# Layer 2's dot features: halves made in node order and turned by one transposing transfer

## The reference, cut to what matters

```python
def _gat_layer(h, mask, b):
    scores = jnp.einsum('...nd,...md->...nm', h, h)
    scores = jnp.where(mask, scores, NEG)
    attn = jax.nn.softmax(scores, axis=-1)
    return jnp.einsum('...nm,...md->...nd', attn, h) + b
h = jnp.einsum('bnc,hdc->bhnd', x, Wh)
out_h = _gat_layer(h, mask[None, None], bh[None, :, None, :])
cat = jnp.transpose(out_h, (0, 2, 1, 3)).reshape(B, N, H * D)
z = jax.nn.leaky_relu(cat, negative_slope=0.2)
h2 = jnp.einsum('bnk,dk->bnd', z, Wo)
out2 = _gat_layer(h2, mask[None], bo)
```

## Time and profile before

| | us |
|---|---|
| median of three runs | 2002.39 (1998.01 to 2004.02) |
| profiled execution | 2003.45 |
| its span in the profile | 2001.6 |
| outside the span | 1.85 |
| mean granted TensorE clock | 0.991 |

### The profile page before, as it was taken

One profiled execution on the slowest core, in us unless ns is written; L12 is line 12 of the kernel. 1 busy time (PEld: TensorE's weight loads), 2 busy tenths in 40 slices (PEclk: granted clock), 3 DMA queues, 4 the chain that ended last, 5 costly groups with the idle time before them and its releaser, 6 DMA issues.

```text
span 2001.6 us, 95064 instructions
## 1 busy us (share of the span) xinstructions
PE 1906.4 (95%) x43624; PEld 1566.2 (78%) x43624; DVE 1681.5 (84%) x1991; ACT 1242.2 (62%) x1886; POOL 1008.6 (50%) x726
## 2 busy tenths in 40 slices
PE   7998898989999999999999999999999999989998
PEld 6787798977777777777777777777777777767887
DVE  6999988767788888888888888888888888867998
ACT  5887655436666666666666666666666666654342
POOL 6676866412354455445454454455435455354653
PEclk8999999999999999999999999999999999999999
DMA  7000000011111111111111111111111111101111
GB/s 182 4 4 4 2 2 2 2 25 33 34 34 35 34 35 34 35 34 31 36 29 32 35 34 35 34 35 34 35 32 29 36 31 34 35 13 25 25 25 35
DMA packets 88255, 61.24 MB, mean 31 GB/s; under 512 B 45616, under 2 KB 86832, under 8 KB 87856
## 3 DMA queue, kind: packets, MB, share of 16 engines
q1 hardware_dynamic: 85632, 54.57, 11.2%
q10 hardware_dynamic: 2224, 0.59, 0.1%
HBM read 8.98 MB, written 4.19 MB: 7 GB/s over the span
## 4 chain that ended last, share of the span: by engine, by line
PE 70%; DVE 14%; ACT 6%; POOL 5%; issue 2%; DMA 1%; SPq 1%; ACTq 0%; POOLq 0%; DVEq 0%
PE ACC L1632 30%; PE S L1813 23%; PE S L1792 6%; DVE ring L1406 5%; PE AX L1856 3%; DVE ring L1259 2%; PE AX L1865 2%; PE AX L1833 2%; POOL sp_log L782 1%; POOL ln_sq L785 1%; ACT ring L1059 1%; DMA FA<-lo 1%; PE AX L1612 1%; DVE ch_rden L1391 1%; ACT st_x L898 1%
## 5 line engine op out<-in xcount | busy, mean ns | idle before, releaser
L1632 PEld LDWEIGHTS ACC<-V,ring 128*64 128x64 f32 x28672 | 955.4, 138 | 179.6 <-DVE ring L1259 34.6
L1406 DVE TENSOR_TENSOR ring<-ring,mask_self_t 128x1024 f32<-128x1024 f32 x640 | 896.0, 1410 | 193.2 <-ACT ring L1059 188.8
L1632 PE MATMUL ACC<-V,ring 128*64 128x65 f32 x28672 | 974.0, 223 | 29.1 <-ACT accs L870 11.9
L1059 ACT ACTIVATE ring<-S,dot_bias 128x1024 f32<-128x1024 f32 x640 | 713.7, 1116 | 414.1 <-PE S L1813 376.0
L1813 PE MATMUL S<-FA 128*64 128x512 f16 x5120 | 666.0, 382 | 4.7 <-DMA FA<-lo 4.6
L1813 PEld LDWEIGHTS S<-FA 128*64 128x64 f16 x5120 | 253.7, 110 | 164.7 <-ACT ring L1059 16.0
L1259 DVE SCALAR_TENSOR_TENSOR ring<-S,pair_q,mask_t 128x1024 f32<-128x1024 f32 x256 | 315.2, 1273 | 15.4 <-DVE f_max L1271 4.6
L798 POOL TENSOR_TENSOR EV_both<-score,recip 128x512 f32<-128x512 f32 x64 | 124.3, 1942 | 323.2 <-DVE score L1415 323.1
L1792 PE MATMUL S<-parts,mask_t 128*128 128x128 bf16 x3072 | 176.1, 221 | 10.8 <-DVE X L1395 10.6
L1792 PEld LDWEIGHTS S<-parts,mask_t 128*128 128x128 bf16 x3072 | 175.0, 99 | 11.8 <-issue 11.8
L791 POOL TENSOR_TENSOR V<-v_pairs,bh_bc 128x512 f32<-128x512 f32 x64 | 95.5, 1493 | 120.8 <-ACT v_pairs L1079 120.8
(11 more groups left out here) (134 smaller groups left out, 2044.2 us busy)
## 6 DMA issues: line engine op xcount, KB each, us to landing
FA<-hi SPq DMA_DIRECT2D x320, 64.0 KB, 2.0
FA<-lo SPq DMA_DIRECT2D x320, 64.0 KB, 2.0
X<-in_x SPq DMA_DIRECT2D x16, 256.0 KB, 5.0
ring<-in_adj SPq DMA_DIRECT2D x8, 512.0 KB, 8.1
out_x<-X SPq DMA_DIRECT2D x16, 256.0 KB, 2.6
wh<-in_wh_t ACTq DMA_DIRECT2D x2, 64.0 KB, 6.5
bh_bc<-in_bh ACTq DMA_DIRECT2D x1, 128.0 KB, 9.4
w_gat<-in_w_gat ACTq DMA_DIRECT2D x4, 16.0 KB, 3.8
```

Source lines behind the costliest of these rows:

```text
L1059: act.activation(ring[:, jt, :], S[jt % 2][:, :], ACT.Exp, bias=dot_bias[:, n % 2:n % 2 + 1])\
L1406: dve.tensor_tensor(ring[:, jt, :], ring[:, jt, :], mask_self_t[:, jt, :], ALU.mult)\
L1632: last = pe.matmul(acc_of(t)[rows, :], ring[:, jt, t * P + c * CUT:t * P + (c + 1) * CUT], values, start=(jt == 0 and t % 4 == 0), stop=(j ...
```

## The change

Both halves are made in node order, with nodes on the partitions, in one array `HL` of 128 x 8 tiles x (64 `hi` + 64 `lo`). ACT makes `hi` in step 0, straight from `AX`, ahead of the copy to `v_pairs`. DVE makes `lo` in step 1, from `v_pairs` and `hi`, ahead of the norms. SP issues one transposing transfer of 256 KB that writes plane 0 of `FA`, waits for it, and copies its two partition halves crosswise to plane 1, 128 KB each. The four turns on PE, ACT's step-2 copy, DVE's step-3 subtraction and the bank job `F` are gone.

```diff
-        hi = sb("hi", [P, 2, HALF], F16)
-        lo = sb("lo", [P, 2, HALF], F16)
+        HL = sb("HL", [P, 2, T, 2 * D], F16)
...
-            return 16 * 8 * (u["n"] // 2 + 1)
+            return 16 * 2 * (u["n"] // 2 + 1)
...
             for u in UNITS:
                 par = buf_of(u)
-                moved = features_in[par]
-                sp.wait_ge(hi_made, u["n"] + 1)
-                for half in range(2):
-                    cols_of = slice(half * HALF, (half + 1) * HALF)
-                    own = slice(half * D, (half + 1) * D)
-                    sp.dma_start(FA[0:D, par, 0, cols_of], hi[own, par, :]).then_inc(moved, 16)
-                    sp.dma_start(FA[D:P, par, 1, cols_of], hi[own, par, :]).then_inc(moved, 16)
                 sp.wait_ge(lo_made, u["n"] + 1)
-                for half in range(2):
...
-                    sp.dma_start(FA[D:P, par, 0, cols_of], lo[own, par, :]).then_inc(moved, 16)
-                    sp.dma_start(FA[0:D, par, 1, cols_of], lo[own, par, :]).then_inc(moved, 16)
+                sp.dma_start_transpose(out=FA[:, par, 0, :].rearrange("p (t n) -> p t n", t=T),
+                                       in_=HL[:, par, :, :].rearrange("p t n -> p (t n)")).then_inc(stacked[par], 16)
+                sp.wait_ge(stacked[par], 16 * (u["n"] // 2 + 1))
+                sp.dma_start(FA[0:D, par, 1, :], FA[D:P, par, 0, :]).then_inc(features_in[par], 16)
+                sp.dma_start(FA[D:P, par, 1, :], FA[0:D, par, 0, :]).then_inc(features_in[par], 16)
...
# ScalarE, values(u)
+                if u["n"] >= 2:
+                    act.wait_ge(stacked[buf_of(u)], 16 * (u["n"] // 2))
+                act.activation(halves_of(HL[:, buf_of(u), :, 0:D]), V_FULL, ACT.Copy).then_inc(hi_made, 1)
                 wait(act, v_made, u["n"])
+                wait(act, lo_made, u["n"])
                 act.activation(v_pairs, V_FULL, ACT.Copy).then_inc(v_copied, 1)
...
                 act.wait_ge(v_copied, u["n"] + 1)
+                act.wait_ge(hi_made, u["n"] + 1)
...
-            def features(u):
...
-                act.activation(hi[:, buf_of(u), :], AX[k][:, :], ACT.Copy).then_inc(hi_made, 1)
...
# VectorE
             def feature_rest(u):
-                k, at = AX_AT["F", u["n"]]
                 par = buf_of(u)
                 dve.wait_ge(hi_made, u["n"] + 1)
-                dve.tensor_tensor(lo[:, par, :], AX[k][:, :], hi[:, par, :], ALU.subtract).then_inc(lo_made, 1)
-                dve.wait_ge(lo_made, u["n"] + 1)
-                dve.sem_inc(ax_free[k], 1)
+                dve.wait_ge(v_copied, u["n"] + 1)
+                dve.tensor_tensor(halves_of(HL[:, par, :, D:2 * D]), v_pairs, halves_of(HL[:, par, :, 0:D]), ALU.subtract)\
+                    .then_inc(lo_made, 1)
...
                 if jt == 1 and nxt:
+                    feature_rest(nxt)
                     norms(nxt)
-                if jt == 3 and nxt:
-                    feature_rest(nxt)
...
# TensorE
-            def features(u):
-                pe.wait_ge(v_copied, u["n"] + 1)
-                k = take_bank(AX_AT["F", u["n"]])
-                for q in range(T // 2):
-                    last = pe.transpose(AX[k][:, q * P:(q + 1) * P], v_by_pair[:, q * P:(q + 1) * P], ident[:, :])
-                last.then_inc(ax_full[k], 1)
...
-                if jt == LAG - 1 and after(u):
-                    features(after(u))
```

More of the change, by code:

```diff
@@ L273, in gnn_stack @@
         lo_made = sem("lo_made")
+        stacked = [sem("stacked0"), sem("stacked1")]
         features_in = [sem("features_in0"), sem("features_in1")]
@@ L404, in place_values @@
                 place(("V", u["n"], half), half)
-        def place_features(u):
-            place(("F", u["n"]), 1)
         def place_bound(u):
@@ L421, in gnn_stack @@
         place_values(UNITS[0])
-        place_features(UNITS[0])
         place_bound(UNITS[0])
@@ L426, in gnn_stack @@
                 place_values(after(u))
-                place_features(after(u))
                 place_bound(after(u))
@@ L448, in gnn_stack @@
         place_values(LAST)
-        place_features(LAST)
         place_bound(LAST)
@@ L1083, in values @@
                 act.wait_ge(v_copied, u["n"] + 1)
+                act.wait_ge(hi_made, u["n"] + 1)
                 for k in range(2):
                     act.sem_inc(ax_free[k], 1)
-            def features(u):
-                k, at = AX_AT["F", u["n"]]
-                act.wait_ge(ax_full[k], at + 1)
-                if u["n"] >= 2:
-                    act.wait_ge(features_in[buf_of(u)], moved_by(UNITS[u["n"] - 2]))
-                act.activation(hi[:, buf_of(u), :], AX[k][:, :], ACT.Copy).then_inc(hi_made, 1)
             def turned(b, chunk):
@@ L1123, in first_features @@
                 values(UNITS[0])
-                features(UNITS[0])
             def dot_layer():
@@ L1147, in last_layer @@
                 values(LAST)
-                features(LAST)
                 gat_sums(3, 1)
@@ L1486, in features @@
             def features(u):
+                feature_rest(u)
                 norms(u)
-                feature_rest(u)
             def dot_layer():
@@ L1522, in last_layer @@
                     if jt == 3:
+                        feature_rest(LAST)
                         norms(LAST)
-                    if jt == 5:
-                        feature_rest(LAST)
                     if jt == 6:
@@ L1750, in last_layer @@
                         values(LAST)
-                    if jt == 2:
-                        features(LAST)
                     if jt == 4:
```

3 lines of the change are left out of this document (removed).

## The result

| | before | after |
|---|---|---|
| median, us | 2002.39 (1998.01 to 2004.02) | 2009.34 (2005.97 to 2012.19) |
| span of the profiled execution, us | 2001.6 | 2007.1 |
| mean granted TensorE clock | 0.991 | 0.992 |

The ratio is 1.0037, with an interval of 1.0028 to 1.0046: slower by 7 us, a little more than the 0.3% that this measurement can tell from no change.

A forecast was written before the change was run, and what follows sets the result against it. PE's order of work was taken to bound layer 2. Terms +26 (POOL collisions), -4 (plain units), -4 (transfer waits), -2 and -1 (first, last unit) gave +15: 2018 us profiled, median 2017; range 1987 to 2130.

The forecast's parts named there:

- rival 2: Only one of the two POOL collisions happens; 26 us become 8 to 17; 2000 to 2009 us, chance 0.15.
- this case: The prediction's own case, both POOL collisions happening: 2017 us, own range 2008 to 2027, chance 0.38.
- The norms hold PE: PE waits at `spread_bound` for `norm_max`; two plain unit kinds keep only 0.15 and 0.1 of 0.69 us, -4 in all.
- POOL's port: DVE instructions with two SBUF inputs, `lo` among them, are held by POOL in two unit kinds: +26 us.
- the kind of the earlier trace: First use: units with L791, PE 0.6 us later; second: units with L548 and L551, 1.24 later; 14 units each.
- near 2 us as a sign: Sign in the profile after: step 1's weights on DVE take near 2 us in units with L548.
- The unit that the prediction calls head 2's: Unit whose norms start later for other DVE work: 0.7 us of cover, gains nothing.
- The transfers: They land in time; `lo` made in step 1 removes waits for its transfers, -4 of 5.7 us.
- X: Transposing transfer's time from issue to landing: taken as 4 us, ends 2.6 and 8.1; may be 5.2 in the tightest unit.
- rival 4: Transposing transfer late, each unit's first `dots` waits: from X = 5.2 on; 2044 us at 6, 2175 at 8; chance 0.29.
- First and last unit: Layer 1's last step loses PE's wait and turns ahead of L1792, -2 us; layer 2's last unit -1.
- if nothing else held PE: Without the four turns PE would save 0.69 us a unit over 80 units: 55 us.

The follow-up runs named there:

- experiment 1: The changed kernel with DVE's norms made ahead of `lo`, nothing else: 1974.99 us, ratio 0.987 to the kernel before.
- Experiment 2: The changed kernel with `lo` read from PSUM in place of `v_pairs`, still ahead of the norms, DVE handing the banks back: 1998.2 us, ratio 0.9986.
- experiment 9: The changed kernel, `lo` still ahead of the norms, with POOL's `stat_rstd` moved behind the values in the next unit: 2000.56 us, ratio 0.9993.
- Experiment 4: The kernel before without the four turns, `hi` and `lo` made at their old places from unturned `v_pairs`, features wrong: 1973.84 us, ratio 0.9865.
- experiment 5: The changed kernel with norms first, `hi` made in step 2 behind the sums and `lo` in step 2 behind the weights: 1986.64 us, ratio 0.9927.
- experiment 7: The changed kernel with norms first and ACT's copy of the old sums ahead of step 2's exponential: 1967.26 us, ratio 0.9825.
- experiment 10: The changed kernel with norms first, old sums ahead of step 2's exponential, POOL's `stat_rstd` and `stat_center` moved behind the values: 1974.49 us, ratio 0.9859.
- experiment 3: The changed kernel with norms ahead of `lo` and `lo` read from PSUM, DVE handing the banks back: 2001.6 us, ratio 1.0005.

## Why the prediction was right, and where it was off

The forecast was 2017 us, its own range 2008 to 2027; 2009.34 lies at its low edge, as good as on the upper end of rival 2's 2000 to 2009, so the time alone can't tell the two. The trace can: both collisions happen, in 13 units each, so it is this case and not rival 2. The slowing came out half of what was forecast, +7 us for +15.

- **The norms hold PE.** Right: L1598 got a wait that it never had, and experiment 1 takes it away and gains 33 us. In a plain unit 0.24 to 0.25 us were kept where I had 0.15 (and 0.17 for 0.1 in the other plain kind). Of this the median periods show 0.19 and 0.11; their sum, -3.7 for my -4.
- **POOL's port.** Right in kind, for `lo` and for both units. Experiment 2 (no `lo` held, though with a hand-back added) and experiment 9 (one of the two taken away) show it. By size: for the kind of the earlier trace rows I took 0.6 as a middle between 0.87 and -0.15. L777 went first, and it was 0.84 at `spread_bound`; +11.6 for my +8.4. For the kind of the earlier trace rows I had 1.24 and it was 0.78, +6.6 for my +17.4. **This is the term that was mis-sized.** I let DVE's weights be held to 4.8 by L548 as in the earlier trace rows; L534, as it is now called, started at 2.27 after the first copy, earlier than the 2.65 I counted with, and so the weights took 1.40 (1.40 or 1.41 in 11 of 14 units, where I had named near 2 us as a sign) and ended at 4.39 in place of my 4.8; L537 ended at 5.29, not 5.7, and `lo` behind it at 5.83, not 6.3. Part of the sum is also that the wait of the earlier trace rows was in this kind and went, with 3.8 of the 5.7 us of the earlier trace rows. I had 14 collisions of each, there are 13.
- **The unit that the prediction calls head 2's (head 3's).** I had 0; it gave -4.1, 0.24 us a unit in the period though `spread_bound` starts only 0.07 earlier. What sets this period is not `spread_bound`: PE waits in it, ahead of the turns of head outputs (L1833, now L1807), for the bank that DVE's `norm_all` in step 4 frees, and DVE is busy from `out_var` up to there. So where `lo` stands in between is all one. What went is a pause behind `lo`, which DVE made to hand bank 1 back. `recip`, the next instruction behind `lo`, starts 8.99 after the first copy before and 8.76 after. Three rows of before, then one of after:

```profile
1085.01 0.68 DVE L1423 TENSOR_TENSOR lo<-AX,hi 128x512 f16<-128x512 f32 x1
1085.84 0.20 DVE L1414 RECIPROCAL recip<-accs 128x8 f32<-128x8 f32 x1
...
1088.09 1.06 PE L1833 MATMUL AX<-ident,EV_both 128*128 128x128 f32 x8 [1.35 <-DVE norm_all L1439]
...
1086.43 0.20 DVE L1393 RECIPROCAL recip<-accs 128x8 f32<-128x8 f32 x1
```

  Before, 0.15 us are idle between `lo` and `recip`; after, `recip` follows the weights with none. Experiment 4, which keeps `lo` in step 3 but has no bank to hand back, has 8.76 and the same period, 18.34; so have experiments 1, 5, 7, 9 and 10, within 0.01, with `spread_bound` anywhere from 5.28 to 5.84. Experiments 2 and 3, with a hand-back behind `lo`, have 18.66 and 18.71.
- **The transfers.** X is 3.1 (3.0 to 4.9) for my 4, under the 5.2 at which rival 4 begins; waits for DMA fell by 5.0 for my 4. For the turning itself, over the 2.6 of a plain transfer of the same bytes, 0.5 us. Of the two figures of the Trainium skill, that of "DMA: Bandwidth & Descriptors" (Latency and other measured facts), 261 GB/s, is of the right order: seven blocks more cost 3.1 - 2.4 = 0.7 us, 0.1 us for 32 KB, some 330 GB/s (an estimate). The 1309 ns a block of "VectorE: DVE Perf Modes" (The three transpose paths) does not hold for blocks of one transfer; it is near what one issue takes on SP's queue here (1.23 us), and eight separate ones do cost that each.
- **First and last unit.** -3.6 for my -2, which were the wait and the turns of the earlier trace rows and came to 2.1. The other 1.6 are the clock that PE lost before and keeps after, 12.51 against 10.89 us for the same 192 matmuls; the prediction had no term for it. -1.3 for my -1.
- **What the removal is worth.** The prediction has 55 us "if nothing else held PE", and says of the copy of the old sums that it holds PE "less than this does, and is covered by it". That step is wrong in part: the copy takes 0.57 us in a plain unit on its way (76.5 us in all against 31.6), and `norm_max` only the rest. Since the two waits follow each other and the later one set the time, the plain units came out right anyway. But experiments 1 and 4 show that with the norms out of the way 25 to 27 us are to be had, not 55; experiment 7 gets 34 to 35.
- **Two slips of the sums.** 13.2 - 4.8 - 3.1 is 5.3 and not 5.2, and the lateness at X = 7.3, worked out as for 6 and 8, gives 2124 and not 2130. Neither touches the forecast.

The sum by measured terms: 11.6 + 6.6 - 3.7 - 4.1 - 3.6 - 1.3 = +5.5, for my +15. The difference of 9 us is -10.8 in the unit with L548, +3.2 in that with L791, +0.3 in the plain ones, -4.1 in head 3's and -1.9 in the first and last; +4 come back, as the waits for DMA, which I counted by themselves, lie within the units here. That the total lies in the range is in part luck: the missing terms of -4.1 and -1.6 and the overrated collision all pull the same way, and a little more would have made it rival 2's number.

## What to carry to other kernels

Work taken off the bounding engine was worth only as much as its next two waits allowed: for each one ask how long its releaser had been done, in the kernel as changed. Before a change is given up as slower, look at the order within the engine that releases: here two lines swapped turned +0.4% into -1.3%. An instruction that comes to read two operands from SBUF on VectorE must be laid beside GpSimd's timeline, and so must what GpSimd moves to when it is shifted.

## What the hardware showed that I had not expected

- A transposing transfer, SBUF to SBUF, of 256 KB of f16 (eight blocks of 128 x 128) lands 3.1 us after its issue, one of 32 KB 2.4; each keeps SP's queue for about 1.23 us, a plain one for 0.46 to 0.60.
- Of VectorE and GpSimd whoever comes second is held nearly to the end of the other's instruction, when both read two operands from SBUF: `lo` took 1.52 and 1.76 us in place of 0.68 (mean of 80: 1026 ns with both inputs in SBUF, 681 with one in PSUM). It goes both ways. In experiment 9 L777, begun at 1090.82, took 2.25 us in place of 1.27, since the weights before it ran to 1091.93; it ended at 1093.07 and held the next weights, begun at 1092.49, to 1094.16. The Trainium skill's rule that the prediction quoted ("Advanced Engine Details and Errata", GPSIMD Details) agrees; the sizes are these runs'.
- TensorE, idle for 1.51 us ahead of the four turns before the first unit, had a granted clock of 0.50 from 409.2 to 412.6, and the 192 matmuls there took 12.51 us in place of 10.89. Without the turns the clock stayed at 1.00. A removal can give back more than the removed work.
- A wait that the profile labels "issue" can be one for another engine's copy out of the same PSUM bank; it is found by the timeline, at the end of that copy (here 78 waits, 45.9 of the 76.5 us).
